# Rows of a batched outer product in chunks of 64, 128 and 8 instead of 64, 64, 64 and 8, with four output slots instead of six

## The reference

```python
# feature: (512, 200, 64) float32, weight: (200, 64, 64) float32
bilinear = jnp.einsum('bie,ied->bid', feature, weight)
out = jnp.einsum('bid,bjd->bij', bilinear, feature)     # (512, 200, 200)
```

## Time and profile before

| | |
|---|---|
| median of 3 runs | 316.3 us (315.22 to 317.37) |
| profiled execution, its own time | 315.12 us |
| its span, first to last instruction | 313.3 us |
| PE busy (MATMUL) | 238.1 us, 76% of the span |
| DVE busy, ACT busy | 151.0 us, 128.0 us |
| moved by DMA | 115.63 MB, mean 369 GB/s |
| time of the packets of the data queue | 92.3% of 16 engines' span |
| mean granted TensorE clock | 0.95 |

### The profile page before, as it was taken

How to read it: one execution, slowest core, us unless ns; L and a number is a source line. 1 busy time by engine, 2 the same in 40 slices (tenths; PEclk the granted TensorE clock), 3 DMA queues, 4 the chain that set the end, 5 groups by cost and what they waited for, 6 DMA issues and landing times.

```text
span 313.3 us, 14575 instructions
## 1 busy us (share of the span) xinstructions
PE 238.1 (76%) x6784; PEld 210.7 (67%) x6784; DVE 151.0 (48%) x176; ACT 128.0 (41%) x177; POOL 2.0 (1%) x5
## 2 busy tenths in 40 slices
PE   0076776999986976799869776999875775999950
PEld 0074676978876866677668675977875775978940
DVE  0033534636772763536546455445565455736640
ACT  1022334444553444244535344344454453544630
POOL 2000000000000000000000000000000000000000
PEclk9996879899997999999988999799999999999995
DMA  7999999798999999998899999988899999677996
GB/s 249 428 410 443 403 409 377 248 371 342 341 381 408 415 410 411 420 368 322 328 386 394 415 414 405 367 349 320 332 353 401 413 411 391 242 311 298 378 411 285
DMA packets 25708, 115.63 MB, mean 369 GB/s; under 512 B 4272, under 2 KB 4272, under 8 KB 25264
## 3 DMA queue, kind: packets, MB, share of 16 engines
q1 hardware_dynamic: 25648, 114.71, 92.3%
HBM read 32.77 MB, written 81.92 MB: 366 GB/s over the span
## 4 chain that ended last, share of the span: by engine, by line
PE 76%; issue 14%; DMA 4%; SPq 1%; DVE 1%; ACT 0%
PE psum L253 49%; PE psum L224 17%; PE psum L270 8%; DMA w_sb<-w_dram 4%; SPq L136 1%; PE psum L236 1%; DVE tile L285 1%; ACT mixed L306 0%
## 5 line engine op out<-in xcount | busy, mean ns | idle before, releaser
L253 PE MATMUL psum<-x_sb,mixed 64*64 64x200 f32 x3072 | 169.2, 355 | 22.3 <-issue 20.1
L253 PEld LDWEIGHTS psum<-x_sb,mixed 64*64 64x64 f32 x3072 | 136.9, 141 | 38.9 <-issue 27.4
L285 DVE COPY tile<-psum 128x800 f32<-128x800 f32 x100 | 99.2, 992 | 102.2 <-PE psum L253 92.9
L285 ACT COPY tile<-psum 128x800 f32<-128x800 f32 x100 | 82.6, 827 | 82.0 <-PE psum L253 63.8
L224 PE MATMUL psum<-x_sb,w_sb 64*64 64x64 f32 x3072 | 65.5, 227 | 39.1 <-issue 21.7
L224 PEld LDWEIGHTS psum<-x_sb,w_sb 64*64 64x64 f32 x3072 | 64.0, 140 | 42.2 <-issue 40.8
L306 DVE COPY mixed<-psum 64x512 f32<-64x512 f32 x48 | 33.1, 689 | 29.1 <-PE psum L224 27.9
L306 ACT COPY mixed<-psum 64x512 f32<-64x512 f32 x48 | 27.8, 580 | 40.8 <-PE psum L224 40.2
L308 ACT COPY mixed<-psum 128x512 f32<-128x512 f32 x24 | 14.1, 587 | 48.5 <-PE psum L224 48.5
L270 PE MATMUL psum<-x_sb,tails 128*32 128x200 f32 x512 | 25.2, 343 | 0.2 <-issue 0.2
L308 DVE COPY mixed<-psum 128x512 f32<-128x512 f32 x24 | 16.6, 690 | 17.4 <-PE psum L224 17.4
## 6 DMA issues: line engine op xcount, KB each, us to landing
out_dram<-tile SPq DMA_DIRECT2D x192, 400.0 KB, 5.6
x_sb<-x_dram SPq DMA_DIRECT2D x64, 400.0 KB, 7.1
w_sb<-w_dram SPq DMA_DIRECT2D x2, 2048.0 KB, 16.3
out_tail_dram<-tile SPq DMA_DIRECT2D x8, 400.0 KB, 3.6
w_sb<-w_dram SPq DMA_DIRECT2D x1, 2304.0 KB, 21.2
```

What stands on the lines that cost most here:

```text
L253: last = nc.tensor.matmul(psum[half_rows(pair), n % BANK_PAIRS * 2 + h, a * FIELDS:(a + 1) * FIELDS], mixed[half_rows(h), (CHUNKS * g + c) ...
L285: copy(tile[:, k % SLOTS, engine], psum[:, bank:bank + 2, 0:2 * FIELDS]).then_inc(copied[engine], 1)
```

## The change

The first 64 fields stay a chunk (*low*), worked as before. Fields 64 to 191 become one chunk of 128 (*high*). In a high unit the mixed rows of 128 fields are the weights of a matmul with 64 rows, 128 weight columns and 200 moving columns, so one sample fills all 128 PSUM partitions; a unit is one quad, 4 matmuls, and again two units fill an 800 KB tile. A group has 8 low tiles, 1 tail tile and 16 high tiles.

All eight mix units of the high chunk now stand in the low stage, after the units (t, u) of `HIGH_MIX_AFTER`; then follow tail_mix and the two tail units, directly after each other; the four low mix units of the next group stand in the high stage. `mixed_low` and `mixed_high` have one buffer each (48 KB a partition where `mixed` had 32 KB), and `tile` has 4 slots instead of 6. The weights come in 13 loads of 16 fields (the last of 8), part 0 in 8 loads of 64 partitions x 6,400 bytes instead of 128 x 3,200. Part 0 of the next group is loaded after the low tiles, part 1 after every second high unit pair, with its load issued ahead of that tile's stores.

```diff
-CHUNK, CHUNKS = 64, 3
+LOW, HIGH = 64, 128
...
-MIX_AFTER = (1, 3, 5, 6)
-TAIL_MIX_AFTER = 6
...
-TAIL_AFTER = (2, 4)
-SLOTS = 6
...
+HIGH_MIX_AFTER = ((1, 1), (3, 1), (4, 1), (5, 0), (5, 1), (6, 0), (6, 1), (7, 0))
+TAIL_MIX_AFTER = (7, 1)
+LOW_MIX_AFTER = ((3, 1), (6, 1), (9, 1), (12, 1))
...
+SLOTS = 4
...
     for g in range(GROUPS):
...
+        for t in range(LOW_TILES):
+            for u in range(2):
+                low(n, g, t, u)
+                n += 1
+                if (t, u) in HIGH_MIX_AFTER:
+                    high_mix(n, g, HIGH_MIX_AFTER.index((t, u)))
                     n += 1
+                if (t, u) == TAIL_MIX_AFTER:
+                    tail_mix(n, g)
+                    n += 1
...
+        for e in range(2):
+
+            tail(n, g, e)
+            n += 1
+        for t in range(HIGH_TILES):
+            for u in range(2):
+                high(n, g, t, u)
+                n += 1
+                if (t, u) in LOW_MIX_AFTER and g + 1 < GROUPS:
+                    low_mix(n, g + 1, LOW_MIX_AFTER.index((t, u)))
                     n += 1
...
+                if kind == "high" and t % 2 == 1 and g + 1 < GROUPS:
+
+                    sp.wait_ge(unit_ready, NUMBER["high", g, t, 1] + 1)
+                    load_part1(sp, g + 1, t // 2)
...
+                if kind == "low":
+                    store(k, out_low[g, t])
+                    if g + 1 < GROUPS:
+
+                        load_part0(sp, g + 1, t // STRIPS, t % STRIPS)
...
+            def high(n, g, t, u):
+                if t == 0 and u == 0:
+                    wait_copies(NUMBER["high_mix", g, HIGH_MIXES - 1])
+                quad = 2 * t + u
+                for pair in range(2):
+                    for h in range(HALVES):
+                        if pair == 0:
+                            wait_bank(n, h)
+                        last = nc.tensor.matmul(
+                            psum[:, n % BANK_PAIRS * 2 + h, pair * FIELDS:(pair + 1) * FIELDS],
+                            mixed_high[half_rows(h), quad, :, pair],
+                            x_sample(g, h, quad, pair), start=True, stop=True)
                 last.then_inc(unit_ready, 1)
```

More of the change, by code:

```diff
@@ L38, with walk @@
+LAST_WAITED = HIGH_MIX_AFTER[CROSSING][0]
+SLOTS = 4
 STRIPS = 2
 STRIP_STORES = STRIPS * 16
-W_PIECES = ((0, CHUNK), (CHUNK, 2 * CHUNK), (2 * CHUNK, FIELDS))
+W_PIECES = FIELDS // MIX_FIELDS + 1
+TAIL_PIECE = W_PIECES - 1
 def half_rows(h):
     return slice(h * EMB, (h + 1) * EMB)
-def next_chunk(g, c):
-    return (g, c + 1) if c + 1 < CHUNKS else (g + 1, 0)
-def walk(score, tail, mix, tail_mix):
+def walk(low, high, tail, low_mix, high_mix, tail_mix):
     n = 0
-    for m in range(MIX_UNITS):
-        mix(n, 0, 0, m)
+    for m in range(LOW_MIXES):
+        low_mix(n, 0, m)
@@ L125, in build @@
     zeroed = sem("zeroed")
[L126 removed]
+    w_loaded = [sem(f"w_loaded{n}") for n in range(W_PIECES)]
     part0_loaded = [sem(f"part0_loaded{b}") for b in range(2)]
@@ L146, in load_w, with store @@
             def load_w(n):
[L147 to L152, removed]
+                fields = slice(n * MIX_FIELDS, min((n + 1) * MIX_FIELDS, FIELDS))
+                sp.dma_start(w_sb[:, fields, :], weight[:, fields, :]).then_inc(w_loaded[n], 16)
+            def store(k, to):
+                for i in range(STRIPS):
+                    sp.dma_start(to[i::STRIPS], tile[i::STRIPS, k % SLOTS]).then_inc(slot_out[k % SLOTS], 16)
@@ L153, in _ @@
+            for b in range(PART0_BLOCKS):
+                for i in range(STRIPS):
+                    load_part0(sp, 0, b, i)
+            for n in range(LOW_MIXES):
+                load_w(n)
             for p in range(PIECES):
                 load_part1(sp, 0, p)
[L155 to L158, removed]
-                for e in range(2):
[L160 to L171, removed]
+                if p in (1, 3):
+                    load_w(LOW_MIXES + p // 2)
@@ L205, in x_sample, with mix @@
                 return x_sb[half_rows(h), g % 2:g % 2 + 2, quad, :, pair]
[L207 to L216, removed]
+            def mix(n, g, first):
+                if g == 0:
+                    pe.wait_ge(w_loaded[first // MIX_FIELDS], 16)
                 bank = n % BANK_PAIRS * 2
@@ L227, in mix, with low_mix, high_mix @@
                 last.then_inc(unit_ready, 1)
+            def low_mix(n, g, m):
+                if m == 0:
+                    pe.wait_ge(part0_loaded[g % 2], 16 * STRIPS * PART0_BLOCKS * (g // 2 + 1))
+                mix(n, g, m * MIX_FIELDS)
+            def high_mix(n, g, m):
+                if m == CROSSING:
+                    for p in range(LAST_WAITED + 1, PIECES):
+                        wait_part1(g, p)
+                mix(n, g, LOW + m * MIX_FIELDS)
             def tail_mix(n, g):
@@ L240, in tail_mix, with low @@
                 last.then_inc(unit_ready, 1)
-            def score(n, g, c, t, u):
+            def low(n, g, t, u):
                 if t == 0 and u == 0:
-                    wait_copies(NUMBER["mix", g, c, MIX_UNITS - 1])
-                if c == 0 and u == 0 and t <= LAST_WAITED:
+                    wait_copies(NUMBER["low_mix", g, LOW_MIXES - 1])
+                if u == 0 and t <= LAST_WAITED:
                     wait_part1(g, t)
@@ L275, in tail @@
                 last.then_inc(unit_ready, 1)
-            walk(score, tail, mix, tail_mix)
+            walk(low, high, tail, low_mix, high_mix, tail_mix)
         def copies(eng, copy, engine):
             def copy_tile(n, k):
+                eng.wait_ge(unit_ready, n + 1)
                 if k >= SLOTS:
```

103 lines of the change are left out of this document (58 added, 45 removed).

## The result

| | before | after |
|---|---|---|
| median | 315.9 us | 338.9 us (4 runs, 334.1 to 343.9) |
| profiled execution, its own time | 315.1 us | 334.1 us (predicted 326) |
| span | 313.3 us | 332.3 us |
| MATMUL records | 6,784 | 5,760 |
| packets of code | 53 | 45 |

The ratio is 1.063, with a 95% interval of 1.051 to 1.076; it leaves out two disturbed runs that the median counts.

What follows compares the result with a forecast made beforehand. PE's pace was taken as the larger of its work and code's arrival in 256-instruction blocks. Scores from 23.1 us, group 0 to 97.6, groups 1 and 2 to 247.4, the last to 324.2, plus 1.8: 326 us; range 303 to 342.

Steps and rivals of the forecast that it cites:

- DMA at 408 GB/s in every full stretch: High stages: 400 KB at about 408 GB/s takes 1.0 us, a tile 2.0, a high stage 33.0 us.
- Low stage of group 0: First group's low stage, from scores at 23.1 us: 34.2 us long, with the group ending at 97.6.
- The last group: Final group: low stage 32.5 us, tail 7.3, lag 3, then 17 tiles in 34 us; end at 324.2.
- I cost the loss of two slots at the smaller stock alone.: Output slots: a turn of 5.1 to 7.7 us fits DMA's 8 us for four; only the 9 us stock was charged.
- The price of a block: Low stage: 256 instructions cost 5.7 us beside full DMA, 4.5 us for the last 136 MATMUL.
- 7.5 arise in the last group: Final group: 7.5 of the 11 us forecast loss, as its last 17 tiles wait for the tail.
- at the lower level: Mixing on a cold clock: a MATMUL took 27 ns, not 15.
- Those of being right: 45 packets; "issue" idle every 128 MATMUL; DMA below 250 GB/s around tails, full in high stages; low stage 33 to 36 us.
- Two of being wrong: From three signs: low stage under 31 us; DMA below 390 GB/s mid high stage; high tiles over 2.2 us.
- cold tails: Tail units begun on a cold clock, after stalls near 3 us: up to 3 us more each.
- Code comes quicker: Low stage: all blocks cost 4.7 us, the stage 29.4, a group 69.7, the kernel 308; chance of faster 0.24.
- High stage slower through weight loads: High stage: 128-column loads take twice 141 ns, PE needs 40 us against 33, the whole 348; chance 0.08.

## Why the prediction was right, and where it was short

**Right by its mechanism.** PE moves by blocks of 256 instructions (45 packets came, as counted); mixing gathered in the low stage makes that stage 800 MATMUL long whatever their columns; the tail then finds no stock. The landings of the packets and the run with half the matmuls show the first, the moved tail and the rates of 108 to 291 GB/s the second. Low stages were 35.9, 33.8, 34.6 and 31.5 us for 34.2, 34.6, 34.6 and 32.5 predicted, tails 7.1 for 7.3.

**Short by 8 us in the profiled execution** (332.3 against 324.2 of span). By groups: scores began at 23.3, as said (23.1); group 0 took 3.7 us more, group 1 2.3 more, group 2 1.7 more, the last 0.2. The terms:
- *DMA at 408 GB/s in every full stretch.* The high stages of groups 0 to 2 took 35.2, 36.4 and 34.9 us for 33.0. This is the largest, 7.5 us. Of it the mean rate of 388 to 391 behind the first 6 us explains 4.1 by an estimate (each stretch of 29 to 31 us, times the rate missing to 408); the other 3.4 lie in the first 6 us, where DMA comes back from empty.
- *Low stage of group 0*, 35.9 for 34.2: the mean clock in it was 0.83, and DMA stayed full beside its blocks until 7 us before its end.
- *The last group*, 77.0 for 76.8, is in part luck: its low stage was 1.0 us shorter than said, what followed the tail 1.4 longer (38.4 for 37.0).
- *"I cost the loss of two slots at the smaller stock alone."* In the kernel before it cost 6.5 us by itself, part of it where the stock was small.
- *The price of a block.* Its sum was right and so was its direction, cheaper as DMA empties; the 4.5 us taken for the last blocks is not the end of it, packets came down to 3.4 us apart.

**Slips in the working that moved nothing.** "7.5 arise in the last group" should read 8.2 by the prediction's own terms (76.8 less 68.6); 8.5 came. The 27 ns "at the lower level" were read in a stretch for which the profile has the clock at 1.00. A stretch at 0.50 is that of the first 64 score MATMUL, which took 5.6 us, 88 ns each, for 45 at full clock:

```profile
17.41:23.32 5.91, 5.91 (x223) 5.76 (x223) 2.53 (x4) 2.20 (x4) 0.00 (x0) 1.00 1.03 415
27.06:32.67 5.61, 5.61 (x73) 4.13 (x76) 0.99 (x1) 1.65 (x2) 0.00 (x0) 0.50 1.03 438
```

**Its own signs.** Those of being right came, but for groups of 76.6 to 78.2 us instead of 75. Two of being wrong came as well: DMA at 388 and 389 GB/s in two high stages, under the 390 named, and high tiles at up to 2.3 us (36.4 us for 16), over the 2.2. They point at the term that was in fact too small, the high stage, and leave the mechanism of the low stage alone.

**The spread.** The median is 5 us above the profiled execution; cold tails of 8 to 10 us, the risk named in the prediction, occur in other runs' traces (9.9 us at a clock of 0.83). None of the slower executions of the changed kernel has a trace, so that they make this spread is not shown.

**The rivals.** *Code comes quicker* would have needed 5.1 us a block; the group 1 and 2 low stages had 5.4 and 5.5. *High stage slower through weight loads* is excluded by 93 ns a MATMUL. These two groups of the changed kernel, the high matmuls and their weight loads (busy, mean ns), beside the earlier trace rows:

```profile
L302 PE MATMUL psum<-x_sb,mixed_high 64*128 64x200 f32 x1024 | 102.6, 345 | 13.5 <-ACT tile L335 13.4
L302 PEld LDWEIGHTS psum<-x_sb,mixed_high 64*128 64x128 f32 x1024 | 90.3, 191 | 22.9 <-ACT tile L335 20.2
```

A load of 128 columns has a mean of 191 ns, against 141 for 64 and 108 for 32, and is hidden: the Trainium skill's proportional rule ("TensorE: Matmul & The Clock Gate", "LDWEIGHTS (loading the stationary operand)") again does not fit the records, and again changes nothing. Its rule that crossing a block of code is "mostly hidden" ("Runtime: NRT & Kernel Launch", "Instruction fetch mechanics") would have made the changed kernel the faster one, at about 293 us by the prediction's estimate; no run here bears it out.

## What to carry to other kernels

Where PE runs many short matmuls, count its instructions per stage, not only their columns: here 256 instructions, 128 of them MATMUL, cost 5.4 to 5.7 us where DMA moved 370 to 377 GB/s and 4.2 us at 178, and a stage that gathers the short ones is that long whatever their columns. Taking instructions out helps only in the stage where PE is late with code; the wider matmul took them out where DMA was the limit, and the order that it forced put them where PE was late. Before a step that hands over nothing is placed, count the stock of finished tiles that DMA will have at that point.

## What the hardware showed that I had not expected

- PE's waits at the end of a block follow DMA's load less than in proportion: at a mean of 262 GB/s instead of 369 they fell from 43.8 to 33.9 us in all. Packets of code landed 3.4 to 4.1 us apart beside an almost idle DMA, and PE went on 1.2 to 1.6 us after a landing.
- DMA counted as nearly full (share 0.85 to 0.98) moved only 198 to 274 GB/s over the two microseconds of the first load in a high stage, in four kernels, and 400 to 409 afterwards (share 1.02), loads included, in the two of them followed further.
- Halving the columns of a 64-column matmul left its time on PE as it was: 1.13 and 1.17 us for 64 MATMUL.
- A gain in one stage was given back in the next: the high stage shortened from 36.4 to 34.2 us in group 1 (loads behind stores), and the kernel stayed where it was.
